# A four-layer graph network on one core: half of the setup's DMAs issued from ScalarE's queue

## The chip, the core and the metric

The kernel runs on one core of a Trainium2 chip. The core has five engines with an instruction stream each: TensorE (PE), VectorE (DVE), ScalarE (ACT), GpSimd (POOL) and SyncE (SP), and 16 DMA engines that move data between memory and the on-chip buffer. An engine's stream can issue DMAs; the stream then goes on as soon as the DMA is handed over, and a semaphore tells when the data has landed. The metric is the time of one execution in microseconds on the device; the median of the runs counts.

## What is computed

Four graph layers on 6250 nodes with 128 features and 106250 edges, each with a layer norm ahead and a residual around it:

```python
edge_index = jnp.stack([src, dst])
h = jnp.maximum(_layernorm(x), 0.0)
x = x + _L0_gnn_ref(h, src, dst, ...)            # attention with q, k, v, skip and gate
h = jnp.maximum(_layernorm(x), 0.0)
x = x + _L1_gnn_ref(h, edge_index, ...)          # MLP on each edge, weighted convolution
h = jnp.maximum(_layernorm(x), 0.0)
x = x + _L2_gnn_ref(h, edge_index, W1, b1, W2, b2)   # two plain convolutions
h = jnp.maximum(_layernorm(x), 0.0)
x = x + _L3_gnn_ref(h, edge_index, edge_weight, W, a_l, a_r, bias)   # attention by a_l, a_r
```

In the last layer the logit of an edge is a sum of two products, of W x with the vectors a_l and a_r of each of four heads.

## The kernel before

The kernel is written by hand: each stage is a block in which every engine has its own stream, with semaphores between them, and it ends with a barrier of all engines. There is no scheduler; the order of the code is the order on each engine. The stages follow one another: the setup (L136 to L263), node_phase("in"), attend(0), node_phase("gate"), edge_pass and weighted_sums, and so on to node_phase("out"). Node phases go over 49 blocks of 128 nodes in seven groups; edge phases go over 832 tiles of 128 edges.

The change is in the setup alone. There, these are the streams:

- SyncE (L182) issues every DMA: the edge data dst_pt, base_all, src_idx and lo_i (L184 to L188), x in two DMAs, x_nat for 48 blocks of 128 rows and a tail of 106 rows (L190, L192), then `loads`, a list of 32 pairs of buffer and source (L163 to L180, issued at L196), eight attention vectors into `att` (L199), seven pads of zeros that fill the last rows of the tables in memory (L203), and at last src_lo and src_hi, two tables in memory that VectorE has computed from lo_i (L206, L208). Then it waits for all of them (L209 to L213).
- `loads` begins with the weights and biases of the first layer, then those of the second, the wg rows, three columns of `col` (each one value for all 128 partitions), r_mlp, gamma and beta, those of the third layer, and ends with four pieces of w_gat and three columns of wg3, each 128 pieces of 4 bytes. The profile writes wg for both wg and wg3.
- VectorE (L226) clears buffers (`zero` signals s_zero), splits lo_i into a low and a high part, waits for x and the edge data (s_in, L242) and computes `local` and `base` (L244, L245). Then it waits for all loads (s_ld, L247).
- TensorE (L255) waits for all loads too (L258), transposes w_gat (L260), and after a copy on VectorE (L251) multiplies it with `att` (L263); VectorE copies the result (L253).
- GpSimd makes two constants. ScalarE has no part in the setup.

What stands on each semaphore: s_in counts the five DMAs of L184 to L192 without lo_i, s_lo lo_i, s_ld the 32 loads, s_att the attention vectors, s_pad the pads, s_lostored the last two. They are reset at L75, where the barrier is.

Of the kernel before, what the change touches and what calls it, by code (L numbers as in the profile page):

```python
# [31 lines left out]
H = 4  # L32
D = F // H
NB = -(-N // P)
NTAIL = N - (NB - 1) * P
NPAD = NB * P
# [5 lines left out]
ROWS = NPAD + P  # L42
# [36 lines left out]
def gnn_kernel(nc, a, out):  # L79
# [17 lines left out]
    tab_qv = dram("tab_qv", [ROWS, 2 * F])  # L97
    tab_k = dram("tab_k", [ROWS, F])
    tab_ax = dram("tab_ax", [ROWS, F // 2 + F])
    tab_b = dram("tab_b", [ROWS, F // 2])  # L100
    tab_row = dram("tab_row", [ROWS, F])
    tab_wh = dram("tab_wh", [ROWS, F + H])
    tab_er = dram("tab_er", [ROWS, H])
# [4 lines left out]
    with ctx:  # L108
# [27 lines left out]
        with Phase(nc) as cx:  # L136
            wg = sb("wg", [P, 3, F], fp32, cx)
            att = sb("att", [P, 2 * H], fp32, cx)
# [39 lines left out]
                      (row_of["out"][:], bcast(a["L3_gnn_bias"], F))]  # L178
            loads += [(w_of["gat"][:, h * D:(h + 1) * D], a["L3_gnn_W"][h]) for h in range(H)]
            loads += [(wg3[:, k:k + 1], a["L0_gnn_Wg"][k * F:(k + 1) * F, :]) for k in range(3)]  # L180
            with nc.Block() as block:
                @block.sync  # L182
                def _(sp):
                    sp.dma_start(dst_pt[:], a["dst_pt"]).then_inc(s_in, 16)  # L184
                    sp.dma_start(base_all[:], bass.AP(tensor=a["dst_pt"].tensor, offset=0, ap=[[0, P], [1, T]])
                                 ).then_inc(s_in, 16)
                    sp.dma_start(src_idx[:], a["src_pt"]).then_inc(s_in, 16)
                    sp.dma_start(lo_i[:], a["src_run"]).then_inc(s_lo, 16)  # L188
                    sp.wait_ge(s_zero, 1)
                    sp.dma_start(x_nat[:, 0:NB - 1, :], a["x"][0:(NB - 1) * P, :].rearrange("(b p) f -> p b f", p=P)  # L190
                                 ).then_inc(s_in, 16)
                    sp.dma_start(x_nat[0:NTAIL, NB - 1, :], a["x"][(NB - 1) * P:N, :]).then_inc(s_in, 16)  # L192

                    sp.wait_ge(s_zero, 1)
                    for to, of in loads:
                        sp.dma_start(to, of).then_inc(s_ld, 16)  # L196
                    for k, name in enumerate(("L3_gnn_a_l", "L3_gnn_a_r")):
                        for h in range(H):
                            sp.dma_start(att[h * D:(h + 1) * D, k * H + h:k * H + h + 1], a[name][h]).then_inc(s_att, 16)  # L199

                    tabs = (tab_qv, tab_k, tab_ax, tab_b, tab_row, tab_wh, tab_er)
                    for t in tabs:
                        sp.dma_start(t[NPAD:ROWS, :], zero[:, 0:t.shape[1]]).then_inc(s_pad, 16)  # L203

                    sp.wait_ge(s_lo, 18)
                    sp.dma_start(src_lo.rearrange("o (p t) -> (o p) t", t=T), lo_f[:]).then_inc(s_lostored, 16)  # L206
                    sp.wait_ge(s_hi, 2)
                    sp.dma_start(src_hi.rearrange("o (p t) -> (o p) t", t=T), hi_f[:]).then_inc(s_lostored, 16)  # L208
                    sp.wait_ge(s_lostored, 32)  # L209
                    sp.wait_ge(s_ld, 16 * len(loads))  # L210
                    sp.wait_ge(s_att, 16 * 2 * H)
                    sp.wait_ge(s_pad, 16 * len(tabs))
                    sp.wait_ge(s_in, 16 * 5)  # L213

                @block.gpsimd
                def _(pool):
                    nc.gpsimd.iota(iota[:], [[1, P]], base=0, channel_multiplier=0,
                                   allow_small_or_imprecise_dtypes=True).then_inc(s_io, 1)
                    nc.gpsimd.iota(minus_p[:], [[0, 1]], base=0, channel_multiplier=-1,
                                   allow_small_or_imprecise_dtypes=True)  # L220
                    nc.gpsimd.memset(ident[:], 0.0).then_inc(s_io, 1)
                    pool.wait_ge(s_io, 2)
                    nc.gpsimd.affine_select(out=ident[:], in_=ident[:], compare_op=ALU.not_equal, fill=1.0,
                                            base=0, pattern=[[-1, P]], channel_multiplier=1).then_inc(s_io, 1)

                @block.vector  # L226
                def _(dve):
                    nc.vector.memset(x_nat[:, NB - 1, :], 0.0)
                    nc.vector.memset(att[:], 0.0)
                    nc.vector.memset(b_gate[:], 0.0)  # L230
                    nc.vector.memset(zero[:], 0.0).then_inc(s_zero, 1)
                    nc.vector.memset(local[:], 0.0)
                    nc.vector.memset(base[:], 0)
                    nc.vector.memset(one[:], 1.0).then_inc(s_set, 1)
                    dve.wait_ge(s_lo, 16)
                    nc.vector.tensor_scalar(hi_i[:], lo_i[:], 7, None, ALU.logical_shift_right).then_inc(s_hi, 1)
                    dve.wait_ge(s_hi, 1)
                    nc.vector.tensor_scalar(hi_f[:], hi_i[:], 1.0, None, ALU.add).then_inc(s_hi, 1)
                    nc.vector.tensor_scalar(lo_i[:], lo_i[:], P - 1, None, ALU.bitwise_and).then_inc(s_lo, 1)
                    dve.wait_ge(s_lo, 17)  # L240
                    nc.vector.tensor_copy(lo_f[:], lo_i[:]).then_inc(s_lo, 1)
                    dve.wait_ge(s_in, 16 * 5)  # L242
                    dve.wait_ge(s_set, 1)
                    nc.vector.tensor_tensor(local[:, 0:T], dst_pt[:], base_all[:], ALU.subtract)  # L244
                    nc.vector.tensor_copy(base[0:1, 0:T], dst_pt[0:1, :])  # L245

                    dve.wait_ge(s_ld, 16 * len(loads))  # L247
                    nc.vector.tensor_tensor(wgs[:], wg[:, 0, :], wg[:, 2, :], ALU.add)
                    nc.vector.tensor_tensor(wgc[:], wg3[:, 1:2], wg3[:, 2:3], ALU.subtract)
                    dve.wait_ge(s_gatT, 1)  # L250
                    nc.vector.tensor_copy(gatT[:], pW[:, 0, :]).then_inc(s_gatc, 1)  # L251
                    dve.wait_ge(s_wa, 1)
                    nc.vector.tensor_copy(w_of["gat"][:, F:F + 2 * H], pW[:, 1, 0:2 * H])  # L253

                @block.tensor  # L255
                def _(pe):

                    pe.wait_ge(s_ld, 16 * len(loads))  # L258
                    pe.wait_ge(s_io, 3)
                    nc.tensor.transpose(pW[:, 0, :], w_of["gat"][:, 0:F], ident[:]).then_inc(s_gatT, 1)  # L260
                    pe.wait_ge(s_gatc, 1)
                    pe.wait_ge(s_att, 16 * 2 * H)
                    nc.tensor.matmul(pW[:, 1, 0:2 * H], gatT[:], att[:], start=True, stop=True).then_inc(s_wa, 1)  # L263
# [1501 lines left out]
```

## Time and profile before

| | us |
|---|---|
| median of 3 runs | 6289.3 |
| the runs | 6282.28 to 6299.85 |
| the profiled execution's own time | 6298.84 |
| its span, first to last instruction | 6296.7 |

The profile is of one execution. Times in it are microseconds from the start of the span. A timeline row gives the start, the duration, the engine (SPq and ACTq are the queues' own instructions, with DMA issues among them), the line, the operation, and in brackets how long the engine sat idle before it and what released it. The duration of a DMA row is the time that the issuing stream spent on the issue, not that of the transfer. In a table by stage, PEclk is TensorE's granted clock as a share of full speed (1.00 is 2.4 GHz), and the DMA share is the mean busy share of the 16 DMA engines.

### The profile page before, as it was taken

The page shows a single profiled execution, that of the slowest core. Times are in us where ns is not written, and L with a number is a line of the kernel's source. Part 1 is how long each engine was busy: PE and PEld are TensorE (multiplying, and loading weights), DVE is VectorE, ACT ScalarE, POOL GpSimd, SP SyncE. Part 2 cuts the span into 40 slices and gives each one's busy share as a digit, 9 for nine tenths or more (in the row PEclk, how much of TensorE's full clock was granted, in tenths as well). Part 3 has the DMA queues.
Part 4 walks back from the last instruction along what each step waited for, and adds up shares of the span by engine and source line. Part 5 has one row for each costly group of instructions (what it writes and reads, how often), then busy time and mean ns, then how long its engine had stood idle before and what let it go on. Part 6 is the DMA issues. An engine that isn't in the chain of part 4 may idle for free. (4 is left out here: it accounts for less than half of the span.)

```text
span 6296.7 us, 119222 instructions
## 1 busy us (share of the span) xinstructions
PE 4473.6 (71%) x27040; PEld 3715.4 (59%) x27040; DVE 3873.5 (62%) x13515; ACT 2370.8 (38%) x5196; POOL 4077.7 (65%) x4193
## 2 busy tenths in 40 slices
PE   4556555547777776666687788778888857888886
PEld 2555555437777776666554445544444446887776
DVE  4777777655555555888655555465555545666665
ACT  3555555334444444777300000110000035656662
POOL 2777777427777776444477777377777717777773
PEclk8777777656666666889899889889998975555556
DMA  5555555215555555554222222122222213333332
GB/s 154 158 159 158 159 160 161 64 50 155 155 155 155 156 155 151 167 163 145 53 59 60 61 58 57 44 61 60 61 59 58 55 40 59 59 59 58 59 59 49
DMA packets 753306, 624.32 MB, mean 99 GB/s; under 512 B 350902, under 2 KB 646922, under 8 KB 752650
## 3 DMA queue, kind: packets, MB, share of 16 engines
q0 software_dynamic: 153600, 343.79, 21.2%
q1 hardware_dynamic: 591884, 271.77, 16.2%
q8 instruction: 188, 3.08, 0.2%
q14 instruction: 466, 3.82, 0.2%
q10 hardware_dynamic: 7168, 1.85, 0.1%
HBM read 532.42 MB, written 84.51 MB: 98 GB/s over the span
## 5 line engine op out<-in xcount | busy, mean ns | idle before, releaser
L1213 POOL DMA_INDIRECT sum_rows<-tab_row,src_idx x1472 | 1421.2, 966 | 659.4 <-issue 437.1
L1256 PE MATMUL sum_pX<-sum_mask,sum_part 128*128 128x512 bf16 x4998 | 1170.0, 387 | 60.2 <-DVE sum_mask L1316 60.2
L627 POOL DMA_INDIRECT l_rows<-tab_qv,src_idx x832 | 791.2, 951 | 368.1 <-issue 246.1
L627 POOL DMA_INDIRECT l_rows<-tab_wh,src_idx x832 | 787.3, 946 | 370.8 <-issue 249.3
L1356 DVE TENSOR_TENSOR acc<-acc,sum_pA 128x128 f32 x1664 | 475.1, 285 | 852.9 <-PE sum_pA L1288 792.4
L362 POOL DMA_INDIRECT l_rows<-tab_ax,src_idx x832 | 790.1, 950 | 292.0 <-issue 266.7
L1256 PEld LDWEIGHTS sum_pX<-sum_mask,sum_part 128*128 128x128 bf16 x4998 | 499.8, 100 | 596.2 <-issue 100.1
L677 PE MATMUL l_pA<-l_hotA,l_wrow 128*128 128x128 f32 x3328 | 712.9, 384 | 55.5 <-DVE acc L863 51.9
L649 PE MATMUL l_pK<-l_winr,l_hotT 128*128 128x128 f32 (+1 forms) x3328 | 672.1, 341 | 65.9 <-DVE l_logit L771 44.9
L649 PEld LDWEIGHTS l_pK<-l_winr,l_hotT 128*128 128x128 f32 x3328 | 641.7, 286 | 77.9 <-issue 55.5
L677 PEld LDWEIGHTS l_pA<-l_hotA,l_wrow 128*128 128x128 f32 x3328 | 645.1, 288 | 66.5 <-ACT l_hotA L724 32.9
L1224 ACT ACTIVATE sum_turned<-sum_pX 128x512 f32<-128x512 f32 x34 | 20.3, 597 | 1722.7 <-issue 1020.6
L863 DVE TENSOR_TENSOR acc<-acc,l_pA 128x128 f32 x1664 | 473.3, 284 | 234.2 <-PE l_pA L677 180.2
L706 ACT ACTIVATE l_hot<-iota,local 128x128 bf16<-128x128 f32 x1664 | 526.2, 389 | 13.8 <-PEq L75 13.8
L380 PE MATMUL l_pK<-l_winr,l_hotT 128*128 128x64 f32 x1664 | 332.8, 383 | 235.7 <-ACT l_hotT L419 235.7
L1316 DVE TENSOR_SCALAR sum_mask<-sum_code 128x512 bf16<-128x512 bf16 x1666 | 498.3, 311 | 2.3
L724 ACT ACTIVATE l_hotA<-l_hot 128x512 f32<-128x512 bf16 x416 | 259.5, 624 | 582.3 <-PE l_pA L677 582.1
L380 PEld LDWEIGHTS l_pK<-l_winr,l_hotT 128*128 128x128 f32 x1664 | 314.9, 291 | 253.4 <-ACT l_hotT L419 132.9
L1288 PEld LDWEIGHTS sum_pA<-sum_hot,sum_rows 128*128 128x128 f32 x2944 | 395.2, 198 | 92.1 <-DVE sum_hot L1299 31.5
L1288 PE MATMUL sum_pA<-sum_hot,sum_rows 128*128 128x128 f32 x2944 | 407.0, 283 | 32.5 <-DMA sum_rows<-tab_row,src_idx 27.1
L971 POOL TENSOR_TENSOR sum_wrow<-sum_rows,sum_wedge 128x1024 f32<-128x1024 f32 x104 | 214.9, 2066 | 269.1 <-DVE sum_wedge L1058 256.1
L1002 PE MATMUL sum_pA<-sum_hot,sum_wrow 128*128 128x128 f32 x1664 | 255.5, 317 | 164.8 <-POOL sum_wrow L971 103.4
(276 smaller groups left out, 7690.4 us busy)
## 6 DMA issues: line engine op xcount, KB each, us to landing
sum_rows_r<-tab_row SPq DMA_DIRECT2D x3584, 0.5 KB
sum_rows_r<-tab_row ACTq DMA_DIRECT2D x3584, 0.5 KB
l_winr<-tab_k SPq DMA_DIRECT2D x832, 64.0 KB
spill<-l_rows SPq DMA_DIRECT2D x104, 512.0 KB
sum_rows<-spill SPq DMA_DIRECT2D x104, 512.0 KB
l_winr<-tab_b SPq DMA_DIRECT2D x840, 32.0 KB
sum_line<-src_lo SPq DMA_DIRECT2D x104, 256.0 KB
sum_rows<-tab_row,src_idx POOLq DMA_INDIRECT x1472
```

What stands on the lines that cost most here:

```text
L362: nc.gpsimd.indirect_dma_start(rows[:, b * TB + u, :], None, table, bass.IndirectOffsetOnAxis(src_idx[:, t:t + 1], 0)).then_inc(s_rows[b], 16)
L380: last = nc.tensor.matmul(pK[:, b, u, :], hotT[:, b, u, :], winr[:, b * TB + u, :], start=True, stop=True)
L627: nc.gpsimd.indirect_dma_start(rows[:, g % R, u, :], None, table, bass.IndirectOffsetOnAxis(src_idx[:, t:t + 1], 0)).then_inc(s_rows[g % R ...
L649: last = nc.tensor.matmul(pK[:, g % 2, u, :], hotT[:, g % 2, u, :], winr[:, g % WR, u, :], start=True, stop=True)
L677: last = nc.tensor.matmul(pA[:, g % 2, u, :], wrow[:, g % 2, u, :], hotA[:, g % 2, u, :], start=True, stop=True)
L706: last = nc.scalar.activation(hot[:, g % HR, u, :], iota[:], ACT.Square, scale=-1.0, bias=local[:, t:t + 1])
L863: nc.vector.tensor_tensor(acc[:, bass.ds(at[u], P)], acc[:, bass.ds(at[u], P)], pA[:, g % 2, u, :], ALU.add).then_inc(s_add, 1)
L1213: nc.gpsimd.indirect_dma_start(rows[:, g % R, u, :], None, tab_row, bass.IndirectOffsetOnAxis(src_idx[:, t:t + 1], 0)).then_inc(s_rows[g % ...
L1256: last = nc.tensor.matmul(pX[:, k % 2, :], part[:, i, h, :], mask[:, step % MASKS, :], start=h == 0 and i == 0, stop=h == NB - 1 and i == 2)
L1288: last = nc.tensor.matmul(pA[:, q % HOTS, u, :], of[:, u, :], hot[:, q % HOTS, u, :], start=True, stop=True)
L1316: nc.vector.tensor_scalar(mask[:, step % MASKS, :], code[:, k % 2, :], float(h + 1), None, ALU.is_equal).then_inc(s_mask, 1)
L1356: nc.vector.tensor_tensor(acc[:, bass.ds(at, P)], acc[:, bass.ds(at, P)], pA[:, q % HOTS, u, :], ALU.add).then_inc(s_add, 1)
```

## The change

The list of 32 loads is split. SyncE issues the first 16, in the same order. A new stream on ScalarE issues the other 16, from the last to the first, then waits for `zero` to be cleared and issues the attention vectors and the seven pads. SyncE's second wait for `zero` goes. All waits at the end of SyncE's stream and the waits of VectorE and TensorE are as before.

```diff
+            tabs = (tab_qv, tab_k, tab_ax, tab_b, tab_row, tab_wh, tab_er)
             with nc.Block() as block:
+                @block.scalar
+                def _(ae):
+                    for to, of in loads[:len(loads) // 2 - 1:-1]:
+                        ae.dma_start(to, of).then_inc(s_ld, 16)
+                    ae.wait_ge(s_zero, 1)
+                    for k, name in enumerate(("L3_gnn_a_l", "L3_gnn_a_r")):
+                        for h in range(H):
+                            ae.dma_start(att[h * D:(h + 1) * D, k * H + h:k * H + h + 1], a[name][h]).then_inc(s_att, 16)
+                    for t in tabs:
+                        ae.dma_start(t[NPAD:ROWS, :], zero[:, 0:t.shape[1]]).then_inc(s_pad, 16)
+
                 @block.sync
                 def _(sp):
...
-                    sp.wait_ge(s_zero, 1)
-                    for to, of in loads:
+                    for to, of in loads[:len(loads) // 2]:
                         sp.dma_start(to, of).then_inc(s_ld, 16)
-                    for k, name in enumerate(("L3_gnn_a_l", "L3_gnn_a_r")):
-                        for h in range(H):
-                            sp.dma_start(att[h * D:(h + 1) * D, k * H + h:k * H + h + 1], a[name][h]).then_inc(s_att, 16)
-
-                    tabs = (tab_qv, tab_k, tab_ax, tab_b, tab_row, tab_wh, tab_er)
-                    for t in tabs:
-                        sp.dma_start(t[NPAD:ROWS, :], zero[:, 0:t.shape[1]]).then_inc(s_pad, 16)
```

SyncE's stream before, from the three columns of `col` to the end of the setup:

```order
20 L196 DMA col<-in_L_gnn_mlp_b 128x1
21 L196 DMA col<-in_L_gnn_bg 128x1
22 L196 DMA col<-in_L_gnn_alpha 128x1
23 L196 DMA r_mlp<-in_L_gnn_mlp_w 128x64
...
33 L196 DMA wg<-in_L_gnn_Wg 128x1 x3
34 L199 DMA att<-in_L_gnn_a_l 32x1 x4
...
42 L203 DMA tab_er<-zero 128x4
43 L206 DMA src_lo<-lo_f 128x832
44 L208 DMA src_hi<-hi_f 128x832
```

and the same place after:

```order
20 L207 DMA col<-in_L_gnn_mlp_b 128x1
21 L207 DMA col<-in_L_gnn_bg 128x1
22 L207 DMA col<-in_L_gnn_alpha 128x1
23 L210 DMA src_lo<-lo_f 128x832
24 L212 DMA src_hi<-hi_f 128x832
25 L182 UNCONDITIONAL_BRANCH
```

src_lo now follows the 16th load directly; 31 DMAs between them are gone from this stream.

ScalarE's stream after, from its start to its first computation, which stood at the start of the stream before:

```order
0 L183 UNCONDITIONAL_BRANCH
1 L186 DMA wg<-in_L_gnn_Wg 128x1 x3
2 L186 DMA w_gat<-in_L_gnn_W 128x32 x4
3 L186 DMA r_out<-in_L_gnn_bias 128x128
...
11 L186 DMA r_mlp<-in_L_gnn_mlp_w 128x64
12 L190 DMA att<-in_L_gnn_a_l 32x1 x4
13 L190 DMA att<-in_L_gnn_a_r 32x1 x4
14 L192 DMA tab_qv<-zero 128x256
...
20 L192 DMA tab_er<-zero 128x4
21 L182 UNCONDITIONAL_BRANCH
22 L1533 UNCONDITIONAL_BRANCH
23 L1539 ACT_TABLE_LOAD
```

The 31 DMAs stand there ahead of everything, the loads in reversed order.

## Rows read from the trace of the kernel before

**Rows 1.** The page: span, and busy time, share and instructions of each engine.
```profile
span 6296.7 us, 119222 instructions
...
PE 4473.6 (71%) x27040; PEld 3715.4 (59%) x27040; DVE 3873.5 (62%) x13515; ACT 2370.8 (38%) x5196; POOL 4077.7 (65%) x4193
```
**Rows 2.** Stages: window, length, busy time of each engine, PEclk, DMA share, GB/s.
```profile
0.00:42.20 42.20, 1.04 (x3) 0.68 (x3) 6.88 (x18) 0.04 (x1) 0.97 (x8) 1.00 0.62 173
...
5060.00:6297.00 1237.00, 940.81 (x4914) 912.22 (x4913) 760.17 (x2957) 675.04 (x1606) 787.31 (x832) 0.54 0.29 55
```
**Rows 3.** Waits up to 42.2 us: in total, times, longest.
```profile
ACT L1535 <- PEq L75: 42.2, 1, 42.2
```
**Rows 4.** Stages of the setup, columns as in rows 2.
```profile
3.70:14.50 10.80, 0.00 (x0) 0.00 (x0) 2.28 (x4) 0.00 (x0) 0.00 (x0) 1.00 1.01 302
14.50:20.00 5.50, 0.00 (x0) 0.00 (x0) 0.26 (x1) 0.00 (x0) 0.00 (x0) 1.00 0.98 264
23.60:30.80 7.20, 0.00 (x0) 0.00 (x0) 0.00 (x0) 0.00 (x0) 0.00 (x0) 1.00 0.31 83
30.80:34.40 3.60, 0.00 (x0) 0.00 (x0) 0.00 (x0) 0.00 (x0) 0.00 (x0) 1.00 0.47 86
34.40:38.20 3.80, 1.04 (x3) 0.68 (x3) 0.82 (x4) 0.00 (x0) 0.00 (x0) 1.00 0.42 122
```
**Rows 5.** Timeline of the setup, SyncE's queue.
```profile
3.69 10.81 SPq L192 DMA_DIRECT2D x_nat<-in_x  x1
...
22.70 0.43 SPq L196 DMA_DIRECT2D col<-in_L_gnn_alpha  x1
23.17 0.43 SPq L196 DMA_DIRECT2D r_mlp<-in_L_gnn_mlp_w  x1
...
29.34 1.38 SPq L196 DMA_DIRECT2D wg<-in_L_gnn_Wg  x3
...
37.83 0.43 SPq L206 DMA_DIRECT2D src_lo<-lo_f  x1
38.30 0.43 SPq L208 DMA_DIRECT2D src_hi<-hi_f  x1
```
**Rows 6.** The same timeline, VectorE, TensorE and ScalarE.
```profile
1.31 0.27 DVE L231 MEMSET zero<- 128x256 f32 x1
...
10.65 0.59 DVE L241 CAST lo_f<-lo_i 128x832 bf16<-128x832 int32 x1
...
19.74 1.02 DVE L244 TENSOR_TENSOR local<-dst_pt,base_all 128x832 f32<-128x832 int32 x1 [8.50 <-DMA x_nat<-in_x]
...
35.57 0.29 DVE L248 TENSOR_TENSOR wgs<-wg 128x128 f32<-128x128 f32 x1 [14.31 <-DMA wg<-in_L_gnn_Wg]
...
37.78 0.17 DVE L253 COPY w_gat<-pW 128x8 f32<-128x8 f32 x1 [1.39 <-PE pW L263]
...
42.16 1.28 ACT L1535 ACT_TABLE_LOAD   x1 [42.16 <-PEq L75]
```
**Rows 7.** Instructions of line 181: durations in ns, start.
```profile
L181 ACTq DRAIN  x1: 8/8/8, 0.8 to 0.8; - x1
...
L181 DVEq DRAIN  x1: 181/181/181, 37.8 to 37.8; - x1
L181 SPq COMPARE_BRANCH  x1: 38/38/38, 41.2 to 41.2; - x1
L181 SPq DRAIN  x1: 7/7/7, 41.4 to 41.4; - x1
```
**Rows 8.** Timeline of a later stage, issues on the two queues.
```profile
3086.23 13.83 ACTq L1177 DMA_DIRECT2D sum_rows_r<-tab_row  x32
...
3188.77 51.48 ACTq L1177 DMA_DIRECT2D sum_rows_r<-tab_row  x112
...
3195.95 54.36 SPq L1177 DMA_DIRECT2D sum_rows_r<-tab_row  x112
```

## The prediction

> **What bounds the kernel now.** I read the busy lines of the page first, then the stages, then the first 42 us in order of time. No engine is at its limit over the whole span: TensorE is busy for 71% of it, VectorE for 62%, GpSimd for 65% [rows 1]. That matters little here, since the change touches only the setup. The stage table shows that the setup, from 0 to 42.2 us, holds next to no computation (6.9 us on VectorE, 1.0 us on TensorE) while the DMA engines are busy for 62% of the time [rows 2]. All engines wait at its end: ScalarE does nothing until the barrier at 42.2 us [rows 3], and the first of seven groups of rows is normalised behind it. So the setup is a serial prefix of 42.2 us in 6296.7 us, 0.67%, and a microsecond taken from it is a microsecond of the kernel, as long as everything behind the barrier only moves earlier.
>
> Inside the prefix the bound changes twice. Up to about 19.7 us, where VectorE gets x [rows 6], it is the transfer of x and of the four tables of edges: the DMA engines are full (share 1.01 at 302 GB/s from 3.7 to 14.5 us, 0.98 up to 20 us) [rows 4], and SyncE's queue is held on the issue of the tail of x for 10.81 us, until 14.5 us [rows 5]. From there to 38.7 us it is the pace of one queue. SyncE issues one DMA every 0.47 us, and the engines are busy for only 0.31, 0.47 and 0.42 in the three windows of that stretch [rows 4]. Last comes the tail: the issue of src_hi ends at 38.73, the wait for it ends in a branch at 41.2, the drain is at 41.4 and the barrier releases ScalarE at 42.16 [rows 5 to 7].
>
> **The change, part by part.**
>
> *31 issues leave SyncE's queue.* They are 16 of the 32 loads, 8 attention vectors and 7 pads. Before, r_mlp, the first of them, starts at 23.17, and src_lo, the first DMA behind all of them, at 37.83 [rows 5]. That is 14.66 us for 31 issues, 0.473 each. In the new order src_lo follows alpha directly, so it would start at 23.17 and src_hi at 23.64, ending at 24.07. It waits for nothing new: lo_f, what it stores, is there from 11.2 us on [rows 6]. Gross term: -14.66 us, which is also the most that the move can give, since nothing else was taken away.
>
> *31 issues are added to ScalarE's queue.* ScalarE is free, and its queue starts near 0.8 us [rows 7]. The nearest rows are a later stage, where 32 issues on ScalarE's queue take 13.83 us, 0.432 each, and where 112 on SyncE's (54.36 us, 0.485 each) and 112 on ScalarE's (51.48 us, 0.460 each) run at the same time [rows 8]. So two queues hardly slow each other there. 31 issues at 0.43 to 0.48 take 13.3 to 14.9 us and end near 15.5 us if nothing blocks them, well ahead of SyncE's. The wait for the zeros is met at 1.6 us [rows 6], ahead of its place. Cost on the path: 0. If that cover went (a queue blocked up to 14.5 us as SyncE's is), some 25 issues would be left, until 14.5 + 25 x 0.473 = 26.3 us, then a landing of 2.5 us: 28.8 us, still below the bound found next.
>
> *A different wait ends last.* With src_hi early, its own tail would release the barrier at 24.07 + (42.16 - 38.73) = 27.5 us. But the small chain on TensorE and VectorE, hidden before by 4 us, is now later. It waits for all 32 loads. Before, the last load (a column of wg3 in pieces of 4 bytes) ended its issue at 30.72 and the chain began at 35.57, 4.85 us later; the chain ended at 37.95, so it takes 2.38 us [rows 5, 6]. After the change the last loads on SyncE's queue are the three columns of col, again pieces of 4 bytes, issued up to 23.13. With the same 4.85 us the chain starts at 27.98 and ends at 30.36; with a landing of 2.5 us, as src_hi's, it starts at 25.6 and ends at 28.0. Draining and the barrier add some 0.9 us (0.18 of VectorE's drain, 0.75 from the drain at 41.4 to 42.16) [rows 7]. The setup then ends at 31.3 or at 28.9 us: a saving of 10.9 or 13.2 us. I take the first, because the pieces are of the same size.
>
> *The moved transfers now fall into the full stretch.* Before, they ran where the engines were half idle. Now they are issued while x is being moved, and x is what holds SyncE's queue until 14.5 us. No row shows a second queue in that stretch, so I bound the cost. The moved transfers are 1.09 MB by the shapes in the diff (64 KB for most loads, 452 KB for the pads). At the 302 GB/s of the full stretch that is 3.6 us. By the share of the engines' time in the three windows in which they ran, it is 0.31 x 7.2 + 0.47 x 3.6 + 0.42 x 3.8 = 5.5 us [rows 4], which is high by some of the earlier loads that still landed there. The lower bound is 0, if ScalarE's packets get in only after x. I take 4.5 us, between the two ways of counting, but with the longer landing that I took above part of it could be counted twice (the landing of wg3 may hold a backlog), so the value for the net is a little higher than 10.9 - 4.5 = 6.4: I take **7.5 us saved**, with 0 and 14.7 as the ends.
>
> The Trainium skill, in "DMA: Bandwidth & Descriptors", section "Issuing engines are not separate DMA queues", says that DMAs from SyncE, ScalarE and GpSimd run on the same 16 engines and interleave, so that a second issuing engine only saves issue time. By that rule the collision is paid in full (5.5 us at most); without it, 0. No row here shows two queues in a full stretch.
>
> *Nothing else moves.* After the barrier both kernels have the same instructions. ScalarE's table of functions is loaded behind the barrier as before. x lands some 4 us later, near 24 us; VectorE's step on it (1.02 us [rows 6]) and a small copy end before 26 us, before its wait for the loads.
>
> *The sum.* 6298.8 us is the profiled execution's own time (span 6296.7 and 2.1 around it). Less 7.5 it is 6291.3. The median of the three runs is 6289.3, 9.5 lower, so the forecast is 6289.3 - 7.5 = **6281.8**, some 0.12% less.
>
> **The rivals.**
>
> *The issues don't run side by side.* If descriptors of both queues are made one DMA at a time, and x's blocks both, the 31 issues are only interleaved: the last of all issues still ends near 38.7 us and nothing is saved: 6289.3. For it: SyncE's queue was held for 10.81 us by a transfer issued before, so some generator or buffer is full in that stretch [rows 5]. Against it: 0.485 and 0.460 us each with both queues running [rows 8]; one at a time it would be 0.9.
> The Trainium skill's "Perfetto Trace Analysis", section "DMA Instruction — HWDGE (DVE, Sync)", describes a shared generator that is locked for exclusive use by each DMA; read strictly it gives this rival. [rows 8] speak against such a reading for small DMAs; for a long one no row does.
>
> *ScalarE's queue is blocked, or served after x.* Then the moved transfers run from 14.5 us on beside SyncE's, where there is room, and x pays nothing. The chain ends the setup at 28.9 to 31.3 us: 10.9 to 13.2 saved, about 6277.
>
> *The granted clock moves, and the kernel is slower.* TensorE's granted clock is 0.54 in the last stage, near the lower of its two levels (1.2 GHz), and 1.00, the upper, in the setup [rows 2]. If work that starts some 8 us earlier met a lower grant there, 0.52 for 0.54, its 940.8 us busy would grow by 36 us, and with TensorE busy for 76% of that stage some 27 us would show: 6309. It makes the kernel slower than before from about 0.534 down, and by over 0.3% from 0.52. Against it: what the engines do per microsecond behind the barrier is unchanged. The same mechanism can go the other way, to about 6256 at 0.56.
>
> **How the numbers follow.** Forecast (queues run side by side, x pays): 0.64. No saving: 0.10. Blocked or served after x: 0.18. Clock lower: 0.03, clock higher: 0.05. The first three all lie within 14.66 us of the time before, 0.23%, so they are inside 0.3% (18.9 us), about what a measurement of this kernel can tell from no change. The three runs of before spread by 17.6 us (6282.3 to 6299.9), and a median of a few runs moves by perhaps 5; that adds a little to both sides: faster 0.08, within 0.89, slower 0.03. The range takes in the savings from 0 to 14.7 (6274.6 to 6289.3) and 7 us of spread at either end: 6268 to 6296.
>
> **What would show it.** Right: 31 DMAs on ScalarE's queue from about 0.8 us at 0.43 to 0.48 each; the issue of x's tail ending at 18 to 20 instead of 14.5 us; src_lo at 26 to 29 us; the chain at L263 (of before) ending last and the barrier at about 34 to 35 instead of 42.2 us; all later stages as long as before. The collision is wrong if the issue of x's tail still ends at 14.5; the side-by-side issue is wrong if ScalarE's issues take 0.9 us each, or stop for 10 us. The whole is wrong if a later stage changes by more than 10 us, above all together with its granted clock.

## The result, and the profile after

| | us |
|---|---|
| before, median of 8 runs | 6292.8 (6280.2 to 6309.3) |
| after, median of 8 runs | 6322.3 (6312.0 to 6343.0) |
| ratio of after to before | 1.0049, 95% interval 1.003 to 1.0067 |
| the profiled execution after, and its span | 6325.2, 6323.1 |

The changed kernel is slower, by half a per cent. I had forecast 6281.8 with a range up to 6296, so the sign is wrong. Eight of the runs below (mid_load, mid_load2, two_pads, one_line, lines2, lines16, dose and one_load3) took 8427 to 8530 us, as did the kernel before beside them (8467.1 and 8526.4), and of them I use no time but those of single issues and, of one_load3, the ratio to before and the length of a convolution.

The setup did about what was forecast. The timeline of the changed kernel, SyncE's and ScalarE's queues and the engines behind them (start, duration, engine, line, operation):

```profile
0.76 1.39 ACTq L186 DMA_DIRECT2D wg<-in_L_gnn_Wg  x3
...
3.69 13.18 SPq L204 DMA_DIRECT2D x_nat<-in_x  x1
...
18.93 0.49 ACTq L192 DMA_DIRECT2D tab_er<-zero  x1
...
25.12 3.18 SPq L207 DMA_DIRECT2D col<-in_L_gnn_bg  x1
25.61 1.02 DVE L248 TENSOR_TENSOR local<-dst_pt,base_all 128x832 f32<-128x832 int32 x1 [13.22 <-DMA x_nat<-in_x]
...
28.34 0.51 SPq L207 DMA_DIRECT2D col<-in_L_gnn_alpha  x1
28.89 0.43 SPq L210 DMA_DIRECT2D src_lo<-lo_f  x1
...
33.58 0.29 DVE L252 TENSOR_TENSOR wgs<-wg 128x128 f32<-128x128 f32 x1 [6.45 <-DMA col<-in_L_gnn_alpha]
...
35.09 0.17 DVE L257 COPY w_gat<-pW 128x8 f32<-128x8 f32 x1 [0.69 <-PE pW L267]
36.02 1.28 ACT L1539 ACT_TABLE_LOAD   x1 [36.02 <-PEq L75]
```

The barrier comes at 36.02 instead of 42.16 [rows 6]: 6.1 us saved, 7.5 forecast. The first gather behind the first node phase starts at 109.73 instead of 116.74. All of that and more is lost later, in the two convolutions of the third layer. Each issues 736 gathers on GpSimd (L1213 before, L1217 after). These rows of before (first) and after give durations in ns (smallest, median, largest) and the first and last start, by convolution:

```profile
L1213 POOL DMA_INDIRECT sum_rows<-tab_row,src_idx x736: 940/944/1797, 3063.0 to 4015.4; - x184
L1213 POOL DMA_INDIRECT sum_rows<-tab_row,src_idx x736: 940/944/1797, 4104.1 to 5056.4; - x184
```
```profile
L1217 POOL DMA_INDIRECT sum_rows<-tab_row,src_idx x736: 940/944/1801, 3042.6 to 4013.5; - x184
L1217 POOL DMA_INDIRECT sum_rows<-tab_row,src_idx x736: 938/944/1802, 4107.8 to 5078.6; - x184
```

The gathers take as long as before, but from the first to the last it is 970.9 and 970.8 us instead of 952.4 and 952.3. I measure a convolution from its first gather to the first matmul of the node phase behind it (4046.5 and 5088.1 before, 4048.2 and 5114.0 after). That gives 983.5 and 984.0 us before, 1005.6 and 1006.2 after: 22 us lost in each, 44 in all, of which the setup gives 6 back. The other stages add up to some 12 us less than before in these two executions (the first convolution starts 20.4 us earlier, not 6.1). I take that for scatter: over the kernels below, with setups of 36 to 43 us, that start lies between 3027 and 3065 us. The two stretches that I can account for, 44 longer and 6 shorter, make 38 us; the medians differ by 29.5, and the interval of the ratio spans 19 to 42.

Within a convolution, ScalarE's and SyncE's queues each issue 1792 DMAs of a single row (L1177 before, L1181 after, both counted for the two convolutions together; ns, smallest, median, largest). Before, then after:

```profile
L1177 SPq DMA_DIRECT2D sum_rows_r<-tab_row x3584: 224/228/307, 3067.2 to 5036.5; - x200
L1177 ACTq DMA_DIRECT2D sum_rows_r<-tab_row x3584: 213/213/530, 3086.2 to 5058.3; - x200
```
```profile
L1181 SPq DMA_DIRECT2D sum_rows_r<-tab_row x3584: 224/228/307, 3046.7 to 5058.7; - x200
L1181 ACTq DMA_DIRECT2D sum_rows_r<-tab_row x3584: 227/228/546, 3065.9 to 5083.6; - x200
```

SyncE's issues are as they were. ScalarE's rose from 213 to 228 ns, the smallest with the median, so nearly every one of them. The code of these issues is the same in both kernels. ScalarE's queue was the later of the two already before (its last issue at 5058.3, SyncE's at 5036.5). The same 112 issues that took 51.48 us [rows 8] now take 53.48:

```profile
3065.89 53.70 ACTq L1181 DMA_DIRECT2D sum_rows_r<-tab_row  x112
...
3171.14 53.48 ACTq L1181 DMA_DIRECT2D sum_rows_r<-tab_row  x112
```

That is 0.4775 us a row for 0.4596, with the pauses between chunks of 16 rows in it. This stretch overstates the difference. Within a chunk the step from one issue to the next is 370 ns before and 384 after, in the median of the trace. Two rows of four issues each, before and after:

```profile
3205.01 1.32 ACTq L1177 DMA_DIRECT2D sum_rows_r<-tab_row  x4
```
```profile
3204.81 1.38 ACTq L1181 DMA_DIRECT2D sum_rows_r<-tab_row  x4
```

Fifteen ns 1792 times are 27 us. Added up over a convolution, all steps shorter than 2.5 us (the 16 longer ones are left out) make 821.7 and 822.0 us before, 848.2 and 847.8 after: the queue has 26 us more to do in each. I call this sum the queue's work below.

Who waits for the queue stands in the list of waits (total us, times, longest); before, then after:

```profile
DVE acc L1356 <- PE sum_pA L1288: 792.4, 337, 19.5
...
PE sum_pA L1288 <- DMA sum_rows_r<-tab_row: 180.0, 14, 20.0
...
POOL sum_rows L1213 <- PE sum_pA L1288: 48.3, 38, 11.0
```
```profile
DVE acc L1360 <- PE sum_pA L1292: 862.0, 341, 21.6
...
PE sum_pA L1292 <- DMA sum_rows_r<-tab_row: 201.0, 14, 21.9
...
POOL sum_rows L1217 <- PE sum_pA L1292: 88.3, 40, 14.4
```

TensorE waits longer for the 14 groups of rows that the two queues bring, VectorE for TensorE, and GpSimd has to hold its gathers until TensorE has read the buffers. How the queue's work turns into the length of the convolution I read from the experiments below, not from these sums.

### The profile page after: what moved, and what is told of

Same layout as the page of the kernel before. It is cut to its first block and busy times, and to the rows that moved or that the text cites. A ratio compares the mean times of both kernels' runs of the same rounds, so it can differ in the third digit from the quotient of the medians.

```text
span 6323.1 us, 119058 instructions
## 1 busy us (share of the span) xinstructions
PE 4461.8 (71%) x26876; PEld 3718.1 (59%) x27040; DVE 3870.5 (61%) x13515; ACT 2371.4 (38%) x5196; POOL 4074.3 (64%) x4193
## 5 line engine op out<-in xcount | busy, mean ns | idle before, releaser
L1217 POOL DMA_INDIRECT sum_rows<-tab_row,src_idx x1472 | 1418.9, 964 | 701.2 <-issue 436.4
L1260 PE MATMUL sum_pX<-sum_mask,sum_part 128*128 128x512 bf16 x4834 | 1154.5, 388 | 70.9 <-DVE sum_mask L1320 61.6
L464 DVE TENSOR_TENSOR l_pre<-l_rows,l_pK 128x512 f32<-128x512 f32 x104 | 71.5, 687 | 487.1 <-DMA l_rows<-tab_ax,src_idx 481.3
```

The source lines that it names most:

```text
L1217: nc.gpsimd.indirect_dma_start(rows[:, g % R, u, :], None, tab_row, bass.IndirectOffsetOnAxis(src_idx[:, t:t + 1], 0)).then_inc(s_rows[g % ...
L1260: last = nc.tensor.matmul(pX[:, k % 2, :], part[:, i, h, :], mask[:, step % MASKS, :], start=h == 0 and i == 0, stop=h == NB - 1 and i == 2)
```

## The experiments

The theory after the result has two steps. **State**: what was issued before on ScalarE's queue makes its later single-row issues dearer. **Pace**: the convolutions wait for the pace of that queue. The rivals are that the number of DMAs matters (volume), that ScalarE's later instructions stand elsewhere in memory (placement), that the earlier end of the setup itself shifts something, and, for the second step, that something other than the pace made the convolutions longer.

### One DMA is enough, instructions that are no DMA do nothing

Four kernels, each the kernel before with one edit. A load of 128 partitions, from ScalarE's queue:

```diff
+                @block.scalar
+                def _(ae):
+                    to, of = loads[24]
+                    ae.dma_start(to, of).then_inc(s_ld, 16)
...
-                    for to, of in loads:
+                    for to, of in loads[:24] + loads[25:]:
```

> The kernel before with one of the 32 loads (r_out, memory to buffer, 128 partitions) issued from ScalarE's queue in the setup, the other 30 moved DMAs still on SyncE's. The changed kernel lost 33 us in the two convolutions: there each single-row DMA on ScalarE's queue takes 228 ns to issue for 213 before, 1792 of them in each. State theory (an earlier DMA on that queue that names other buffers leaves the issues dearer): 227 to 228 ns here too, each convolution about 1005 us for 983. Volume theory (it takes the whole of the 31 DMAs): 213 ns and 983 us. Placement theory (the later instructions of ScalarE's stream stand elsewhere in memory): 213 or something between, since only a few instructions are added.

One pad, to the table that the convolutions read (one_row, shown) or to another, tab_er (one_er); SyncE leaves it out:

```diff
+                @block.scalar
+                def _(ae):
+                    ae.wait_ge(s_zero, 1)
+                    ae.dma_start(tab_row[NPAD:ROWS, :], zero[:, 0:tab_row.shape[1]]).then_inc(s_pad, 16)
```

> The kernel before with one pad (zeros to tab_row) on ScalarE's queue in the setup. tab_row is the table that the convolutions' DMAs on this queue read. State theory in its form that names count (a table of addresses that the queue has met): 213 ns, 983 us, since only the buffer of zeros is new; in its form that any multi-partition DMA on the queue is enough: 228 ns, 1005 us.

> The kernel before with one pad (zeros to tab_er) on ScalarE's queue in the setup. It names a table in memory that this queue did not name before. State theory by names: 228 ns, 1005 us for each convolution; if the direction decides (loads, not stores): 213 ns and 983 us.

No DMA, but waits:

```diff
+                @block.scalar
+                def _(ae):
+                    for _ in range(33):
+                        ae.wait_ge(s_zero, 1)
```

> The kernel before with 33 waits on a semaphore that is already met, and no DMA, at the start of ScalarE's stream. They shift all later instructions of the stream by as many places as the changed kernel does. Placement theory: 228 ns for each single-row issue on ScalarE's queue, 1005 us for each convolution. State theory: 213 ns, 983 us.

The rows of ScalarE's queue in one_load, one_row, one_er and waits33, in this order:

```profile
L1182 ACTq DMA_DIRECT2D sum_rows_r<-tab_row x3584: 227/228/550, 3050.5 to 5066.4; - x200
```
```profile
L1183 ACTq DMA_DIRECT2D sum_rows_r<-tab_row x3584: 227/228/550, 3058.2 to 5074.0; - x200
```
```profile
L1183 ACTq DMA_DIRECT2D sum_rows_r<-tab_row x3584: 227/228/539, 3072.7 to 5088.3; - x200
```
```profile
L1182 ACTq DMA_DIRECT2D sum_rows_r<-tab_row x3584: 213/213/536, 3062.8 to 5039.3; - x200
```

| | issue, ns | convolutions, us | span, us |
|---|---|---|---|
| before | 213 | 983.5, 984.0 | 6296.7 |
| after | 228 | 1005.6, 1006.2 | 6323.1 |
| one_load | 228 | 1004.0, 1005.9 | 6303.9 |
| one_row | 228 | 1004.0, 1005.8 | 6313.2 |
| one_er | 228 | 1003.5, 1006.1 | 6327.6 |
| waits33 | 213 | 984.4, 985.8 | 6277.5 |

The spans are of one execution each and scatter: eight executions of the kernel before took 6280 to 6309 us. The convolutions scatter little. A single DMA of 128 partitions in the setup costs both convolutions nearly all that the 31 cost them (20.0 to 22.1 us for 22.1 and 22.2), whether it loads or stores, and whether or not it names the table that the queue reads later. Volume falls, and so does the form of the state theory that goes by names. Placement falls too, with one limit: the 33 waits were folded into 16 instructions, half of the shift that I had meant. But one_load adds next to nothing but its one DMA to ScalarE's stream and shows the whole effect. The setup of one_load, one_row and one_er ends at 41.1 to 42.5 us (42.16 before), so no earlier end of the setup is needed for it either.

The granted clock is a rival for the growth. These rows give the two convolutions of before and then of one_load, with the columns as in rows 2:

```profile
3063.00:4046.50 983.50, 775.96 (x4231) 470.71 (x4232) 546.36 (x1905) 32.20 (x48) 710.64 (x736) 0.89 0.23 57
4104.10:5088.10 984.00, 773.33 (x4231) 468.57 (x4232) 545.69 (x1905) 32.30 (x48) 710.58 (x736) 0.90 0.23 57
```
```profile
3027.20:4031.20 1004.00, 775.83 (x4232) 470.82 (x4232) 543.30 (x1905) 32.29 (x48) 710.42 (x736) 0.88 0.22 56
4090.90:5096.80 1005.90, 778.75 (x4231) 473.34 (x4231) 544.41 (x1905) 32.30 (x48) 710.41 (x736) 0.88 0.21 56
```

The clock of TensorE is a little lower, 0.88 for 0.89 and 0.90, but its busy time changes by 0 and by 5 us while the convolutions grow by 20 and by 22. What grows is its waiting.

The kernel of one_load again, in five executions beside eight of the kernel before (6288.1 in the median):

> The kernel before with one load of 128 partitions on ScalarE's queue in the setup. State theory: 228 ns, convolutions of 1004 to 1006 us, +42 us less what the setup changes (it was 1 us longer in the first look): ratio 1.005 to 1.007. If the loss came from the many DMAs or from the earlier end of the setup: 1.000.

Its ratio to before was 1.006 (1.0037 to 1.0084), with issues of 228 ns and convolutions of 1003.2 and 1006.1 us. That fits the changed kernel's loss without the setup's saving; the intervals of the two ratios overlap, so the times alone don't tell them apart.

### The switch within one execution

The kernel before, with one more load, of values that the buffer already holds, placed between the convolutions:

```diff
+                        if kind == "mid":
+                            ae.dma_start(row_of["out"][:], bcast(a["L3_gnn_bias"], F)).then_inc(s_x, 16)
...
+                        if kind == "mid":
+                            ae.wait_ge(s_x, 16)
```

> The kernel before with one more DMA, a load of the last layer's bias of 128 partitions (it writes the same values again), on ScalarE's queue between the two convolutions. State theory in any form in which what was issued before decides: the issues in the first convolution stay at 213 ns and those of the second take 228; the first lasts about 983 us, the second 1005. If only the setup matters (what is issued at the start of the program): 213 and 983 in both.

> Again the kernel before with one load of 128 partitions on ScalarE's queue between the two convolutions. State theory: the first convolution at 213 ns and 984 us, the second at 228 ns and 1005 us, in one execution. If the setup alone decides: 213 and 984 in both.

> The kernel before with one load of 128 partitions on ScalarE's queue between the two convolutions. State theory: the second convolution at 228 ns and 1005 us. The first was seen at 217 ns per issue, which is 4 ns x 1792 = 7 us more for the queue: 984 to 990 us. If the setup alone decides: the second as the first.

mid_load3, the first and the second convolution:

```profile
L1177 ACTq DMA_DIRECT2D sum_rows_r<-tab_row x1792: 217/217/534, 3088.2 to 4024.7; - x200
```
```profile
L1177 ACTq DMA_DIRECT2D sum_rows_r<-tab_row x1792: 227/228/540, 4136.6 to 5088.0; - x200
```

The same line, in one execution, goes from 217 to 228 ns at the load, and a convolution from 989.0 to 1005.4 us. mid_load and mid_load2 showed the same two medians, 217 and 228. So for the step to 228 what has gone through the queue decides, and neither the setup nor its earlier end. The expectation of 213 ns for the first convolution failed in mid_load and mid_load2. That step, 217 for 213, I can't explain: nothing had been issued on the queue ahead of the first convolution in either kernel. The program only contains one more DMA. So a small part of the price goes with the program and not with what was issued.

### What about the DMA

two_pads issues the pads of tab_row and tab_er, 128 partitions each, from ScalarE's queue. The other three cut the pad of tab_row: its last m rows go to ScalarE's queue and the rest stays on SyncE's (m is 1, 2 and 16 in one_line, lines2 and lines16; the wait for the pads counts one more):

```diff
+                    ae.wait_ge(s_zero, 1)
+                    ae.dma_start(tab_row[ROWS - m:ROWS, :], zero[0:m, 0:F]).then_inc(s_pad, 16)
...
                     for t in tabs:
-                        sp.dma_start(t[NPAD:ROWS, :], zero[:, 0:t.shape[1]]).then_inc(s_pad, 16)
+                        end = ROWS - m if t is tab_row else ROWS
+                        sp.dma_start(t[NPAD:end, :], zero[0:end - NPAD, 0:t.shape[1]]).then_inc(s_pad, 16)
```

> The kernel before with two pads (zeros to tab_row and tab_er, 128 partitions each) on ScalarE's queue in the setup. One such DMA was enough to lift each later single-row issue on that queue from 213 to 228 ns. Any-DMA theory: 228 ns again, each convolution about 1005 us. Parity theory: one DMA of 128 partitions over 16 engines leaves an odd number of entries (8 rows and a semaphore write) in each engine's ring and each single row adds an even number (2), so that every later pair straddles a boundary; two such DMAs bring the ring back to an even place: 213 ns, 983 us.

> The kernel before with a single row (the last row of zeros of tab_row, one partition) issued from ScalarE's queue in the setup; the other 127 rows of that pad stay on SyncE's. Parity theory: an even number of entries, 213 ns, 983 us. Theory that the spread over 16 engines decides: 213 ns too. Theory that any DMA with a fixed address, or any DMA in the setup, decides: 228 ns, 1005 us. The setup may take a few us more, since the 127 rows have another shape.

> The kernel before with 2 rows of zeros (2 partitions) of tab_row's pad on ScalarE's queue in the setup, the other 126 on SyncE's. Theory that a DMA spread over more than one DMA engine decides: 228 ns for each later single-row issue, convolutions of about 1005 us. Theory that it takes all 16 engines, or many rows on one: 213 ns, 984 us.

> As lines2 with 16 rows, one for each DMA engine. Spread theory, also in its form that needs all 16: 228 ns, 1005 us. Theory that many rows on one engine decide, or an odd number of entries in its ring (here each engine gets a row and a semaphore write, as with a single row): 213 ns, 984 us.

> Again the kernel before with one load of 128 partitions on ScalarE's queue in the setup, timed against the kernel before. State theory: the whole loss of the convolutions and none of the setup's saving, +40 to +44 us less what the setup changes: ratio 1.006 to 1.007, above the changed kernel's 1.005. If the loss came from the many DMAs or from the earlier end of the setup: 1.000.

The rows of two_pads, one_line, lines2 and lines16, in this order:

```profile
L1184 ACTq DMA_DIRECT2D sum_rows_r<-tab_row x3584: 3/228/1396, 3710.7 to 6782.4; - x200
```
```profile
L1183 ACTq DMA_DIRECT2D sum_rows_r<-tab_row x3584: 2/213/1398, 3720.8 to 6801.0; - x200
```
```profile
L1183 ACTq DMA_DIRECT2D sum_rows_r<-tab_row x3584: 2/224/1422, 3758.5 to 6874.2; - x200
```
```profile
L1183 ACTq DMA_DIRECT2D sum_rows_r<-tab_row x3584: 2/228/1394, 3774.9 to 6863.9; - x200
```

The smallest and largest are disturbed in these runs, the medians are not. One partition leaves 213 ns, two give 224, 16 and 128 give 228, and so do two DMAs of 128. The trace shows what each of them put on ScalarE's queue: 2 packets for one row, of 512 and of 4 bytes; 4 for two; 32 for 16 (16 of each kind); 144 for a DMA of 128 partitions, 16 of them of 4 bytes. Parity falls: two such DMAs, 288 packets, give 228, and so do the 32 packets of lines16. Many rows per DMA engine aren't needed. What fits is that the number of partitions over which an earlier DMA was spread counts, two being most of the step. Whether it is the partitions, the DMA engines behind them, the number of 4-byte packets (1, 2, 16, 16) or of all packets, I did not separate. Nor are the bytes excluded: 0.5, 1, 2 (the pad of one_er), 8 and 64 KB stand in the same order, though from 2 KB on nothing changes. I had expected 228 or 213 from lines2 and nothing between, so that expectation failed.

one_load3 had 228 ns as well, and yet a ratio of 1.0001 (0.9982 to 1.002); the 1.006 to 1.007 that I had expected did not come. There a convolution lasts some 1560 us. So the dearer issue cost nothing that could be measured there. That something slower than the queue's pace is waited for in those runs would explain it, and is not shown.

### The price of the pace

The kernel before, with a met wait ahead of each row on ScalarE's queue alone:

```diff
                     for i in range(LOAD):
+                        if half:
+                            q.wait_ge(s_line, 16)
                         q.dma_start(rows_r[p0 + i:p0 + i + 1, j % 2, u, :], tab_row[bass.ds(of[i], 1), :]
                                     ).then_inc(s_r[j], 16)
```

> The kernel before with a wait on a semaphore that is long met ahead of each single-row DMA on ScalarE's queue in the convolutions, none on SyncE's; no DMA is moved. It prices the disputed step: does a slower pace on this queue alone cost what the change cost? Between before and after the period of a row rose from 0.462 to 0.479 us and each convolution grew by 22 us, that is 22 us for 1792 rows x 0.017 us = 31 us. If the pace of this queue bounds the convolution, it grows here by 0.7 times 1792 times what the period grows (by 0.02 us: 25 us; by 0.05: 63 us). If something else made the convolutions longer (the clock, or SyncE's queue), they stay at 983 us.

> The kernel before with a wait on a semaphore that is long met ahead of each single-row DMA on ScalarE's queue in the convolutions, no DMA moved; it prices a slower pace of this queue by itself. Pace theory: the period of a row there rises from 0.462 us, and each convolution grows from 983 us by about 0.7 x 1792 x that rise (the change: rise 0.017, growth 22 us), and the ratio to before rises with it. If the pace is not what the convolutions wait for: 983 us, ratio 1.000.

dose, one of the eight, says nothing on the price; dose2, with the same edit, does:

```profile
L1179 ACTq DMA_DIRECT2D sum_rows_r<-tab_row x3584: 213/213/530, 3078.9 to 5083.7; - x200
```
```profile
3182.49 52.65 ACTq L1179 DMA_DIRECT2D sum_rows_r<-tab_row  x112
```

The DMA itself stays at 213 ns; the period, the time from one row to the next in this stretch, grew from 0.4596 to 0.4701 us, 18.8 us in a convolution. They lasted 999.5 and 999.3, 16 and 15 us more. Ratio 1.0074 (1.0048 to 1.01), which is 30 to 63 us; the convolutions account for 31 of them. So a slower pace of this queue alone, with no DMA moved, lengthens the convolutions. By the queue's work (the sum of steps from above), first and second convolution:

| | step, ns | queue's work, us | convolutions, us | grown by, us |
|---|---|---|---|---|
| before | 370 | 821.7, 822.0 | 983.5, 984.0 | |
| mid_load3, first only | 373 | 828.6 | 989.0 | 5.5 for 6.9 |
| dose2 | 380 | 841.3, 841.4 | 999.5, 999.3 | 16.0 for 19.6, 15.3 for 19.4 |
| after | 384 | 848.2, 847.8 | 1005.6, 1006.2 | 22.1 for 26.5, 22.2 for 25.8 |

A convolution grows by some 0.8 us for each us that the queue has more to do, whether a wait or a dearer issue makes it so. The slope of 0.7 that I had expected came from the period of one stretch, whose 0.0179 us overstate what the change did.

The other way round, 2 of the 112 chunks of 16 rows go to SyncE's queue, in the changed kernel:

```diff
+            GIVEN = (41, 89)
...
                                 rows_one_by_one(sp, 0, c)
+                                if c in GIVEN:
+                                    rows_one_by_one(sp, G // 2, c)
...
-                                rows_one_by_one(ae, G // 2, c)
+                                if c not in GIVEN:
+                                    rows_one_by_one(ae, G // 2, c)
```

> The changed kernel, but in each convolution 2 of the 112 chunks of 16 rows that ScalarE's queue issues go to SyncE's, which was done 22 us earlier. The issues stay at 228 ns. Pace theory: ScalarE's queue has 32 rows less, 15.3 us of issues, in each convolution, so each gets up to 15 us shorter (about 995 for 1006) and the kernel 15 to 30 us faster than the changed one: ratio to before about 1.001. If the pace of this queue is not what binds, or SyncE's takes its place: as the changed kernel, 1.005.

```profile
L1182 SPq DMA_DIRECT2D sum_rows_r<-tab_row x3648: 224/228/304, 3043.4 to 5034.9; - x192
L1182 ACTq DMA_DIRECT2D sum_rows_r<-tab_row x3520: 227/228/546, 3062.6 to 5050.9; - x196
```

Issues at 228 ns as in the changed kernel, but 32 fewer on ScalarE's queue: 989.4 and 992.6 us instead of 1005.6 and 1006.2, 16 and 14 us for 15.3 us of issues taken away. The convolutions are still 6 and 9 us longer than before, of 22 each, and the setup is 6 shorter. The ratio to before is 0.9992 (0.9977 to 1.0007): no loss can be told any more, with the state still there. Both steps of the theory stand. One link I can't show: TensorE's 14 waits for the rows add up to 207.2 us here, more than the 201.0 after, while GpSimd's waits for TensorE fall from 88.3 to 53.7. So of these two sums the second follows the length of the convolution and the first does not.

### A setup that leaves the queue alone, and a faster kernel

The last 15 loads from GpSimd's queue, with a semaphore of their own, and ScalarE's queue untouched (pool_q); best adds the two chunks of each convolution given to SyncE's queue, as in after_bal:

```diff
+            by_pool = loads[17:]
+            loads = loads[:17]
...
+                    for to, of in by_pool:
+                        pool.dma_start(to, of).then_inc(s_ldp, 16)
```

> The kernel before with the last 15 of the 32 loads issued from GpSimd's queue in the setup instead of ScalarE's; SyncE keeps the rest, the attention vectors and the pads. ScalarE's queue stays without such a DMA. State theory: its issues in the convolutions stay at 213 ns, 983 us each, and the saving of the setup is kept: 15 issues fewer on SyncE's queue are 7 us, less some for the transfer of x, so 3 to 7 us faster than before, ratio 0.999 to 1.000. A theory in which the earlier end of the setup itself (other phases of the clock) made the convolutions longer: about 1.004.

> The kernel before with both: 15 loads from GpSimd's queue, and 2 of 112 chunks of rows of each convolution moved from ScalarE's to SyncE's queue. Pace and state theories together: issues at 213 ns, setup 3 to 7 us shorter, each convolution up to 10 us shorter: 10 to 25 us faster than before, ratio 0.996 to 0.998, faster than both kernels. If ScalarE's pace does not bind in the kernel before: 0.999.

pool_q, then best:

```profile
39.14 1.28 ACT L1543 ACT_TABLE_LOAD   x1 [39.14 <-PEq L75]
...
L1185 ACTq DMA_DIRECT2D sum_rows_r<-tab_row x3584: 213/213/539, 3071.3 to 5045.1; - x200
```
```profile
L1186 ACTq DMA_DIRECT2D sum_rows_r<-tab_row x3520: 213/213/532, 3080.8 to 5048.8; - x196
```

pool_q ends its setup at 39.14 us, 3.0 earlier than before, and its convolutions last 983.5 and 984.5 us. An earlier end of the setup by 3 us does them no harm. Its ratio is 1.0004 (0.9993 to 1.0015): 3 us are below what can be told. best, with the two chunks moved as well, has 980.2 and 981.5 us and 0.9977 (0.9961 to 0.9993), 6280.7 us in the median for 6295.6 of before beside it. It is the fastest kernel of those that ran several times. Only some 3 us of the gain are seen in each convolution, for 14.5 us of work taken from ScalarE's queue, so there something else soon binds; I did not look for what. With the 2.3 us of its setup (39.83) that makes 8 of the median's 15 us; where the rest is I can't show, and the interval (4 to 25 us) takes in the 8 alone.

## Why the prediction was wrong

*31 issues leave SyncE's queue: right.* src_lo starts at 28.89 (26 to 29 forecast), 5.7 us later than the 23.17 without a collision.

*ScalarE's queue takes them beside its own: right in kind, off in size.* They run from 0.76 to 19.4 us, 0.60 us each on average for 0.43 to 0.48. The queue was slowed where x was moved, not blocked. So neither of the two rivals on the issues (one at a time; blocked until 14.5 us) came true.

*The chain on TensorE and VectorE ends last: right, and its length was misread.* The last load's issue ended at 28.85 and VectorE began at 33.58, 4.73 us later, for 4.85 taken from before. But I took 2.38 us for the chain from before. TensorE waited in it for the attention vectors, which SyncE's queue then issued behind the loads:

```profile
37.18 0.56 PE L263 MATMUL pW<-att,gatT 128*128 128x8 f32 x2 [1.11 <-DMA att<-in_L_gnn_a_r]
```

After, the vectors are long there and the chain takes 1.68 us (33.58 to 35.26). These 0.7 us and smaller ones offset part of the collision. The plain sum of the prediction, 6.4 us, was nearer to the 6.1 measured than the 7.5 taken: the landing had no backlog in it that could have been counted twice.

*The collision: 4.5 us taken, 5.7 measured on SyncE's queue and 5.9 on x (25.61 for 19.74).* On the queue it came in two parts, which I had as one: 2.4 us at the issue of x's tail (13.18 for 10.81; the issue ended at 16.9, where I had forecast 18 to 20), and a stop at the issue of bg, 3.18 us for 0.43. The first part fits the Trainium skill, which says that DMAs of all issuing engines run on the same 16 DMA engines and interleave ("DMA: Bandwidth & Descriptors", section "Issuing engines are not separate DMA queues"). The second part is not shown to be the same thing. It fell from 25.1 to 28.3 us, when ScalarE's queue had nearly nothing left (12 packets from 25.0 to 26.5 us) and all 16 engines moved 23 GB/s. It stands in after_bal too (3.02 us), whose setup is the same, and not in pool_q; its cause is open. The section's other half, that a second issuing engine only saves issue time, holds for the setup and not for the kernel: here it saved 6 us and made later issues dearer, which cost 44.

*"Nothing else moves. After the barrier both kernels have the same instructions": this step failed.* The instructions are the same, but not what they cost. I had the rows of the convolutions' issues on ScalarE's queue before me [rows 8], as the price of an issue, and did not ask what else hangs on that price: 1792 issues in each convolution, on the queue that finishes last. The runs put in its place: one DMA of 128 partitions on ScalarE's queue lifts 1792 later issues by 15 ns in each of two convolutions, 26 us more work for the queue each time, and each convolution grows by 22 us: 44 us, against 6 us saved in the setup. I had named the sign of it myself, a later stage that changes by more than 10 us; the price of it was nowhere in the sum.

*The slower rival was the wrong one.* I gave 0.03 to a lower clock in the last stage. That stage's granted clock did not move (0.54 in both kernels), and it is as long as before (the gathers of the last layer from 5202.4 to 6241.4, 1039.0 us, for 1039.7). A rival on what the moved DMAs leave behind on their new queue was missing altogether, and so my range was bounded by what the setup could do.

## What to carry to other kernels

When a DMA goes to another queue, look for everything that this queue issues later, not only for what it does at that moment; a change of 15 ns matters where thousands of issues on one queue set the pace. If a queue issues single rows in a hot loop, try to leave it without any DMA over several partitions, and compare the smallest and the median issue time before and after. Here two queues shared such a loop, and the one whose last issue came later set its length: in the changed kernel, moving 2 of 112 chunks in each took 30 us off the two convolutions, five times what the setup had saved. In the kernel before the same move gave only some 6 us, so try it and measure.

## What the hardware showed

- The issue of a single-row DMA on ScalarE's queue took 213 ns in the kernels in which that queue has no other DMA, or one more of one partition (before, waits33, dose2, pool_q, best, one_line); 224 after one of two partitions (lines2), 228 after one of 16 or 128 (lines16, one_load, one_row, one_er, after). It lasted to the end of the second convolution, 5000 us later, and over 3584 issues. SyncE's queue, which had carried DMAs of 128 partitions before, was at a median of 225 to 228 in all kernels.
- Before any such DMA, the issue took 217 ns instead of 213 in the kernel in which one stands later in the program (mid_load, mid_load2, mid_load3). Open.
- Two queues issue side by side while the DMA engines are full: 31 DMAs of ScalarE's in 18.7 us beside the transfer of x, whose tail took 2.4 us longer to issue and which landed 5.9 us later.
- The wait for the loads ended 4.85 us (before) and 4.73 us (after) behind the last load's issue, in both kernels a load of 4-byte pieces over 128 partitions.
